# A four-level decoder with mixtures of experts: one rotation of six PSUM banks in the pipelined attention flows, and keyed item sums at the tick's end

## The reference

```
x = norm(x + L0_attn(x))    16 heads of 8, causal, rotary;   x = norm(x + L0_xattn(x, ctx)); x = norm(x + L0_ffn(x))
x = L1_attn(x)              four layers of local and linear attention and MLP
x = norm(x + L1_xattn(x, ctx))  16 heads of 8, keys of ctx;  x = norm(x + L1_ffn(x))
x = norm(x + L2_attn(x))    causal;  x = norm(x + L2_xattn(x, ctx)), made of a1 and a2, attentions with 16 heads of 32
x = norm(x + L2_ffn(x))     one ternary matrix
x = norm(x + L3_attn(x))    masked, with relative keys and values; x = norm(x + L3_xattn(x, ctx)); x = norm(x + L3_ffn(x))
```

## Time and profile before

| | us |
|---|---|
| runs of the kernel before | 4815.51, 4841.33, 4860.01 |
| their median | 4841.33 |
| the profiled execution, its own time | 4883.28 |
| its span in the trace | 4881.6 |
| PE busy | 4182.5 (86%) |
| PEld busy | 2503.5 (51%) |
| ACT busy | 2427.9 (50%) |
| DVE busy | 2337.9 (48%) |
| POOL busy | 521.4 (11%) |

### The profile page before, as it was taken

The page is one execution under the profiler, slowest core; times in us unless marked ns, Lnnn a source line. Parts: engine busy times, 40 slices in busy tenths (PEclk is TensorE's granted clock), DMA queues, the critical chain, the costliest instruction groups (busy, mean ns, idle before and its releaser), DMA issues.

```text
span 4881.6 us, 91781 instructions
## 1 busy us (share of the span) xinstructions
PE 4182.5 (86%) x34405; PEld 2503.5 (51%) x34405; DVE 2337.9 (48%) x6310; ACT 2427.9 (50%) x7589; POOL 521.4 (11%) x619
## 2 busy tenths in 40 slices
PE   7888997999999998887788898788888898778896
PEld 3444484555555466665344444445544444445592
DVE  4555323766766533244444433565455433565323
ACT  3555343666766633322464454554565455564342
POOL 0011241000000002143001100000111100000350
PEclk8888998999999966599789988889789999888996
DMA  5000163000000000045000000000000000000272
GB/s 204 20 11 11 31 205 106 3 12 7 8 8 7 1 4 16 12 128 166 5 1 2 6 6 2 2 2 27 12 10 2 6 6 2 1 1 8 71 225 69
DMA packets 107762, 173.55 MB, mean 36 GB/s; under 512 B 13345, under 2 KB 71969, under 8 KB 107201
## 3 DMA queue, kind: packets, MB, share of 16 engines
q1 hardware_dynamic: 92544, 137.55, 9.3%
q0 software_dynamic: 13632, 28.04, 1.6%
q10 hardware_dynamic: 1152, 2.10, 0.1%
HBM read 115.09 MB, written 52.54 MB: 34 GB/s over the span
## 4 chain that ended last, share of the span: by engine, by line
PE 55%; ACT 19%; DVE 16%; issue 5%; DMA 2%; POOL 1%; another core or an unknown queue 1%; SPq 0%; DVEq 0%; POOLq 0%; ACTq 0%
ACT work L2586 7%; PE bank L1748 5%; PE bank L1825 4%; DVE rowmax L3691 3%; PE bank L1488 3%; PE bank L1499 3%; PE bank L1760 2%; PE bank L1660 2%; PE bank L1743 2%; PE bank L1938 2%; ACT probsT L2321 2%; PE bank L1795 2%; PE bank L1835 2%; PE bank L1777 2%; PE bank L890 2%
## 5 line engine op out<-in xcount | busy, mean ns | idle before, releaser
L3691 DVE TENSOR_REDUCE rowmax<-bank 128x4 f32<-128x512 f32 (+1 forms) x896 | 522.2, 625 | 760.5 <-PE bank L1748 498.5
L2586 ACT ACTIVATE work<-bank,rowmax 128x128 f32<-128x128 f32 x1536 | 539.9, 378 | 256.2 <-PE bank L1825 109.7
L1748 PE MATMUL bank<-km,q 32*128 32x512 f32 (+1 forms) x1280 | 420.3, 738 | 63.8 <-ACT probsT L2571 49.0
L2571 ACT ACTIVATE probsT<-bank 77x512 f32<-77x512 f32 (+1 forms) x512 | 277.0, 592 | 350.2 <-PE bank L1777 330.3
L2586 ACT ACTIVATION_READ_ACCUMULATOR work<-bank,rowmax 128x1 f32 x1536 | 334.1, 218 | 0.0
L1825 PE MATMUL bank<-probsT,vm 128*32 128x128 f32 (+1 forms) x5120 | 257.5, 358 | 22.2 <-DVE qd L3764 7.7
L4122 POOL COPY spread<-small 128x2 f32<-128x2 f32 x48 | 9.1, 189 | 2486.6 <-ACT spreadT L2471 2452.2
L1835 PEld LDWEIGHTS bank<-ident,work 128*128 128x128 f32 x1536 | 208.5, 167 | 105.6 <-issue 98.9
L1835 PE MATMUL bank<-ident,work 128*128 128x128 f32 x1536 | 261.7, 325 | 0.0
L4143 POOL DMA_INDIRECT pair_rows<-qd,dest x234 | 226.4, 967 | 279.6 <-DVE qd L3634 233.3
L2321 ACT ACTIVATE probsT<-bank,rowmax 128x128 f32<-128x128 f32 x512 | 180.5, 364 | 120.9 <-DVE rowmax L3218 119.4
(11 more groups left out here) (427 smaller groups left out, 8493.1 us busy)
## 6 DMA issues: line engine op xcount, KB each, us to landing
slot<-in_w_L_ffn SPq DMA_DIRECT2D x78, 578.0 KB
expert_rows<-slot SPq DMA_DIRECT2D x36, 516.0 KB, 6.4
slot<-in_w_L_ffn SPq DMA_DIRECT2D x39, 450.0 KB
qd<-expert_rows SPq DMA_DIRECT2D x117, 129.0 KB
back<-pair_rows SPq DMA_DIRECT2D x24, 512.0 KB, 4.1
slot<-in_w_stream SPq DMA_DIRECT2D x13, 512.0 KB
pair_rows<-qd,dest POOLq DMA_INDIRECT x234
small<-in_w_small SPq DMA_DIRECT2D x1, 2354.5 KB, 8.5
```

What stands on the lines that cost most here:

```text
L1748: nc.tensor.matmul(b[:, 0:4 * nk], B["q"][c][g32, s * P:(s + 1) * P], km[c][g32, s, :, 0:nk], start=not st["mask"], stop=True).then_inc(*m ...
L2571: nc.scalar.activation(probsT[t % 2][0:nk, r, :, :], banks.where(("keyed", n, c, s, r))[0:nk, :] .rearrange("p (j t) -> p j t", j=4), ACT. ...
L2586: ins = nc.scalar.activation(probs[t % 2][:, r, j, 0:nk], banks.where(("scores", n, c, s, r))[:, j * nk:(j + 1) * nk], ACT.Exp, bias=rowma ...
L3691: ins = V.tensor_reduce(m[:, 4 * r:4 * r + 4], banks.where(("scores", n, c, s, r))[:, 0:4 * nk] .rearrange("p (j k) -> p j k", j=4), AX_X, ...
```

## The change

Four edits. All rings of the flows but "sums" and "rows" become one ring "round" of six banks, used in the order in which TensorE's program takes them. In keyed ticks `totals` is issued in two halves, heads j = 0, 1 before the first `shift` and j = 2, 3 behind it, and `attend` moves to the end of the tick, behind the second `shift`; ScalarE's `invert` moves from the tick's end to stand before its side steps of the first slot. ScalarE's exponentials of unkeyed items wait for the weighted sum of the item two before only where that was of `post` kind. Keys and the first values of the wide heads move one slot earlier, and each flow starts one tick earlier.

```diff
-WIDE_HEAD = [(-6, "keys", (0, 1)), (-5, "keys", (2, 3)), (-4, "values", (0, 1)), (-3, "queries", (0, 1)),
+WIDE_HEAD = [(-7, "keys", (0, 1)), (-6, "keys", (2, 3)), (-5, "values", (0, 1)), (-3, "queries", (0, 1)),
              (-2, "queries", (2, 3)), (-1, "values", (2, 3)), (12, "out", None)]
...
-        self.ticks = range(-3, PER * (len(self.visits) - 1) + last // 2 + 1)
+        self.ticks = range(-4, PER * (len(self.visits) - 1) + last // 2 + 1)
...
-                             "front": (0, 1), "back": (2, 3), "sums": (4,), "rows": (5,), "work": (6, 7),
+                             "round": (0, 1, 2, 3, 6, 7), "sums": (4,), "rows": (5,),
...
-                                b = bank(("scores", n, c, s, r), ("row_max" if keyed(st) else "probs", (n, c, s, r)), "front")
+                                b = bank(("scores", n, c, s, r), ("row_max" if keyed(st) else "probs", (n, c, s, r)), "round")
...
-                                bank(("keyed", st["name"], c, s, r), ("probsT", (st["name"], c, s, r)), "back")
+                                bank(("keyed", st["name"], c, s, r), ("probsT", (st["name"], c, s, r)), "round")
...
-                    def totals(t, st, c, s):
+                    def totals(t, st, c, s, js):
                         n, nk = st["name"], st["nk"]
-                        b = bank(("summed", n, c, s), ("log_sum", (n, c, s)), "rows")
-                        for r in FRONT_ROWS + BACK_ROWS:
-                            pe.wait_ge(*have("probsT", (n, c, s, r)))
-                        for j in range(4):
+                        if js[0] == 0:
+                            bank(("summed", n, c, s), ("log_sum", (n, c, s)), "rows")
+                            for r in FRONT_ROWS + BACK_ROWS:
+                                pe.wait_ge(*have("probsT", (n, c, s, r)))
+                        b = banks.where(("summed", n, c, s))
+                        for j in js:
...
-                        ins.then_inc(*made("summed", (n, c, s)))
+                        if js[-1] == 3:
+                            ins.then_inc(*made("summed", (n, c, s)))
...
                         if past and keyed(past[0]):
-                            totals(t - 2, *past)
+                            totals(t - 2, *past, (0, 1))
                         if past and not keyed(past[0]):
                             turn_spread(t - 2, *past)
+                            attend(t - 2, *past)
                         if prev and keyed(prev[0]):
                             shift(*prev, BACK_ROWS)
-                        if past:
-                            attend(t - 2, *past)
+                        if past and keyed(past[0]):
+                            totals(t - 2, *past, (2, 3))
...
                         if prev and keyed(prev[0]):
                             shift(*prev, FRONT_ROWS)
+                        if past and keyed(past[0]):
+                            attend(t - 2, *past)
...
-                        if rows == FRONT_ROWS:
+                        if rows == FRONT_ROWS and item(t - 2) and item(t - 2)[0]["post"]:
                             attended(t - 2)
...
                             exps_keyed(t - 1, *prev, BACK_ROWS)
+                        if past and keyed(past[0]):
+                            invert(t - 2, *past)
                         others(2 * t)
...
-                        if past and keyed(past[0]):
-                            invert(t - 2, *past)
                         others(2 * t + 1)
```

More of the change, by code:

```diff
@@ L1831, in turn @@
                         for r in rows:
-                            b = bank(("turned", n, c, s, r), (turned_by(st, r), (n, c, s, r)), "back")
+                            b = bank(("turned", n, c, s, r), (turned_by(st, r), (n, c, s, r)), "round")
                             pe.wait_ge(*have("probs", (n, c, s, r)))
@@ L1862, in keys @@
                             freed = "k" if st["rope"] else "k_masked_s"
-                            b = bank((which + "_raw", n, c), (freed, (n, c) if freed != "k_masked_s" else (n, c, 2)), "work")
+                            b = bank((which + "_raw", n, c), (freed, (n, c) if freed != "k_masked_s" else (n, c, 2)), "round")
                             nc.tensor.matmul(b[:, 0:PER * nk], weight(st, which), src, start=True, stop=True
@@ L1876, in queries @@
                         for which in ("q", "qs") if st["rope"] else ("q",):
-                            b = bank((which + "_raw", n, c), ("q", (n, c)), "work")
+                            b = bank((which + "_raw", n, c), ("q", (n, c)), "round")
                             nc.tensor.matmul(b[:, 0:TOK], weight(st, which), src, start=True, stop=True
@@ L1901, in diagonals @@
                         n = st["name"]
-                        b = bank(("diag_raw", n, c), ("diag", (n, c)), "work")
+                        b = bank(("diag_raw", n, c), ("diag", (n, c)), "round")
                         pe.wait_ge(*have("near_prod", (n, c)))
@@ L1954, in down @@
                         n = tagged(name, g)
-                        b = bank(("proj", n, c), ("acc_taken", (n, c)), "work")
+                        b = bank(("proj", n, c), ("acc_taken", (n, c)), "round")
                         for m in range(4):
@@ L2062, in flow @@
                         if not (now or prev or past):
-                            warm(6, "back")
+                            warm(6, "round")
                         others(2 * t + 1)
```

42 lines of the change are left out of this document (21 added, 21 removed).

## The result

The changed kernel takes 4355.47 us (median of 4 runs, 4333.93 to 4374.61) against 4838.2 us for the one before, timed beside it: a ratio of 0.9001 [0.8935, 0.9068], 10% less. Ratios leave out executions that stand clearly above the fastest of their kernel, so they need not be the quotient of two medians. The forecast was 5.5% less, 4575 us, and 4430 us was the low end of its range. The profiled execution took 4341.11 us (span 4339.4) against 4883.28 (span 4881.6): 542 us less.

What follows compares the result with a forecast made beforehand. TensorE binds, losing time by idling and by running at the lower clock. Gains of 387 us less 119 us of losses gave net -268 us: 4615 us profiled, 4575 us as a median; range 4430 to 4745 us, 8 times in 10.

Steps and rivals of the forecast that it cites:

- (2): Rival, chance 0.08: in unkeyed ticks the mask stall moves whole to the weighted sum; 4782 us as a median.
- rival 3: Chance 0.07: in the common ring, late gelu or norm-step releases stop scores; slower, 5213 us as a median.
- (a): Unkeyed ticks: one ring removes 181 us of mask waits, a new weighted-sum wait costs 58; gain 123 us.
- (e): Side steps (up, value and query matmuls) get up to six banks and wait less; gain 48 us.
- (b): Unkeyed ticks: TensorE spends less time at the lower clock level; gain 100 us, bounds 0 to 200.
- rival 1: Chance 0.15: stalls go but TensorE's clock stays, its lower level keeping its share; 4650 us as a median.
- (c): Keyed items' weighted sums at the tick's end no longer wait for VectorE's context; gain 71 us.
- (d): Keyed products of head rows 0 and 1 stop waiting for exponentials of rows 2 and 3; gain 45 us.
- (f): Keyed ticks: key sums split round the first shift may expose ScalarE's copy; loss 13 us, 0 to 69.
- (g): Wide heads half a tick earlier cost 0 us (-15 to +15); flows' extra empty ticks lose 9 us.
- (h): Where TensorE moves ahead, hidden waits for data become visible; a quarter of the gains lost, 97 us.

Runs made afterwards that it cites:

- fill_before: The kernel before with six useless warm-up matmuls ahead of the scores of each unkeyed tick, its bank pairs kept; 4790.24 us, ratio 0.9988.
- either part alone: Two runs: the kernel before with only the one ring of six banks, 0.9216; the changed kernel with the three old bank pairs back, 0.933.
- after_again: The changed kernel run again without edits, in the second session; 4211.81 us, ratio 0.8814 to the kernel before.
- totals_whole: The changed kernel with all four key sums in one piece ahead of the first shift; ratio 0.905 to the kernel before.
- no_ring: The changed kernel with the three old pairs of banks back and all else of the change kept; 4503.17 us, ratio 0.933.

## Why the prediction was right in kind and too small

The direction, the bound and the mechanisms of the waits hold; the clock's reach and the reserve do not. By the numbers of the last part of the prediction: the mask idle fell to 57 us (under 40 was asked for), the sum's wait for L2630 is 49.7 (60), no keyed sum waits for L3770, the up matmuls wait 7.5 (under 20), L2_attn has a clock of 0.91 (0.9) and ticks of 10.4 and 11.2 us (11), the idle in the flows is 233 us (300), ScalarE's exponentials wait for no sum, and L1777 waits 7 us (wrong over 30). Against the rivals: the clock in L2_attn rose (1), the new wait is 50 us and not 150 (2), and no release of a gelu or norm step stands before L1729 or L1748; the largest before L1743 is 2.4 us (3). What rival 3 described is there in small: three masks wait 4.6 us in all for a key step's release (ScalarE's km, L2652).

The 542 us of span, counted by tick from one first row maximum to the next: 96 unkeyed ticks idle 160 us instead of 282 and are busy 132 us less; 128 keyed ticks idle 62 us instead of 221 and are busy 125 us less. That makes 538, and leaves 4 for all the rest. Some of it is scatter: the profiled execution of before lay 45 us above its median and that of after 14 us below, so in medians the change gave 483 us and the forecast missed by 220.

- (a) Mask stall and sum: -123 predicted, -122 measured over all idle of the unkeyed ticks, but by luck, since two errors cancel. The masks keep 57 us that I had at 0, because side steps use up the ring's reach. With the sum's row up from 18.9 to 71.3 us, masks and sum gave only some 71 us; the rest came from side steps, which I had under (e). The sum in (a) also has a slip: its five pieces add up to 3.7 us, not 3.9, which leaves 0.9 us a tick and not 0.7. The wait measured is 49.7 us over 96 ticks, 0.5 us, nearer to the 0.6 that I took.
- (b) The clock in unkeyed ticks: -100 predicted, -132 measured, within its bounds of 0 to 200. The Trainium skill's page "TensorE: Matmul & The Clock Gate", section "A second HAM failure mode: psum-queue depth-cycling", tells of a kernel that cycles through PSUM banks and whose short idles between groups of matmuls make the clock oscillate. The traces agree as far as the idles go, since the clock rose where they shrank or were filled (0.79 to 0.91 here, to 0.92 in fill_before). Cycling through banks did not by itself keep the clock down, as the prediction had read it for rival 1: TensorE still cycles in both.
- (b) again, the first step that failed: it stood "in the same ticks" and gave keyed ticks nothing. They gave 125 us: L2_a1 33, L2_a2 40, L3_ffn 8 and flow 1 44. L2_a1 went from 0.93 to 0.98 and L2_a2 from 0.87 to 0.98 in their first stretches, and either part alone does that to L2_a1 (0.98 with the ring, 1.00 with the order). Flow 1's 44 us are not the change's for certain, since its clock differs between sessions; the other 81 are the step's error. The earlier trace rows had the clue: every flow row stood below the layer stage's 1.00, not only the masked ones.
- (c), (d), (e) and (f), the keyed idle: -71 - 45 - 48 + 13 = -151 predicted, -159 measured for the keyed ticks, again with parts that cancel. (c) gave the 63 us of L1822; the 7.7 us that it added are no keyed sum's but the first one of L3_attn, and they became 10.8. (d) gave 28 us of 49.0 here, 41 in after_again. (e) gave more than it was charged: all idle before the up, value and query matmuls fell from 92 to 15 us, part of it in unkeyed ticks. (f) lost nothing that shows, and by totals_whole its sign may be wrong.
- (g) Heads and empty tick: +9 predicted, nothing measurable.
- (h) Catching up, the second step that failed: "I take a quarter", 97 us. Nothing of it came: the idle fell by 122 + 159 = 281 us where (a) and (c) to (f) had 274 before this reserve. It had no row, and what rows there were spoke against it: in the earlier trace rows ScalarE is busy 60% of the masked stretch, and even in the shorter one after only 75% (125 of 167 us). Such a reserve, taken off a sum whose other steps had rows, was the larger error after the clock.

So of the 274 us between 4615 and 4341 in the profiled executions, 54 of which are their scatter, 133 are the keyed ticks (125 of clock, 8 of idle), 31 the unkeyed ones (32 of clock, less 1), and 110 are (h) and the empty ticks.

What stays open: what decides the clock of flow 1 in a session, why L2_a2 has two times, and whether the split of the key sums gives or costs.

## What to carry to other kernels

Where one engine fills tiles that others drain in a fixed order, try one long ring in place of several short ones: here it took 7.8% by itself, because the engine no longer waits for the tile that it handed over last. Count its reach in takes with the side work in it, since each side take shortens it by one. When TensorE binds and stops waiting, count the gain twice, once as idle and once as clock, and do so for every stage that stands below the upper level; here idle and clock gave 281 and 257 us. A reserve for waits that no row shows needs a reason in the rows. Compare kernels within one session.

## What was not expected of the hardware

In flow 1 the granted clock can stay at one of its two levels for long stretches, and how much of flow 1 each level has differs between sessions for one program. With the order alone (no_ring) it stood at 1.2 GHz (0.50) for 198 us on end. TensorE is busy 39.70 of the 40 us in this window of it:

```profile
1740.00:1780.00 40.00, 39.70 (x426) 27.75 (x422) 10.48 (x33) 11.59 (x29) 0.00 (x0) 0.50 0.01 4
```

In after_again it stood at 2.4 GHz (1.00) for 379 us on end, from 1621 us to beyond the end of flow 1:

```profile
1615.00:1962.00 347.00, 334.67 (x4866) 252.30 (x4867) 182.25 (x646) 154.55 (x377) 122.06 (x153) 1.00 0.28 82
```

A tick of L1_xattn takes 6.3 to 6.5 us there, and 11.1 us in the first half of flow 1 in no_ring, at 0.51. Nothing in the instructions differs between after_again and the changed kernel. This is worth up to 102 us here, 2% of the kernel, and it is most of what moved the kernel's ratio between 0.881 and 0.900. Why the clock stayed down in no_ring with TensorE busy 39.70 of 40 us is not known; idle time cannot be the reason in that window.
